# Order of a round on TensorE: values of two rounds back ahead of scores

## The reference, cut to what matters

```python
q, k, v = (split_heads(x @ W.T) for W in (Wq, Wk, Wv))      # [128, 16, 128, 32]
a = einsum('bhnd,bhmd->bhnm', q, k) * 512 ** -0.5 + 2 * adj[:, None]
a = where(any(a != 0, axis=-1, keepdims=True), a, -inf)
p = softmax(a, axis=-1)                                      # nan becomes 0
o = einsum('bhnm,bhmd->bhnd', p, v)
out = layernorm(x + merge_heads(o) @ Wo.T, eps=1e-5)
```

## Time and profile before

| | |
|---|---|
| median of three runs | 1736.4 us (1736.4 to 1737.27) |
| the profiled execution, its own time | 1735.29 us |
| its span in the profile | 1733.5 us |
| TensorE's granted clock, mean | 0.998 of full |
| busy: PE, VectorE, ScalarE, GpSimd | 99%, 92%, 79%, 55% |

### The profile page before, as it was taken

One profiled execution on the slowest core, in us unless ns is written; L12 is line 12 of the kernel. 1 busy time (PEld: TensorE's weight loads), 2 busy tenths in 40 slices (PEclk: granted clock), 3 DMA queues, 4 the chain that ended last, 5 costly groups with the idle time before them and its releaser, 6 DMA issues. The chain is left out here.

```text
span 1733.5 us, 45700 instructions
## 1 busy us (share of the span) xinstructions
PE 1708.4 (99%) x14370; PEld 1379.8 (80%) x14370; DVE 1589.5 (92%) x5815; ACT 1368.2 (79%) x5134; POOL 962.1 (55%) x1516
## 2 busy tenths in 40 slices
PE   9899999999999999999999999999999999999996
PEld 7788888888888888888888888788888888888884
DVE  7999999999999999999999999999999999999996
ACT  7787788788778877887788788778877887888775
POOL 2255556555555555565555555555655556556543
PEclk9999999999999999999999999999999999999999
DMA  6677777777777777777777777777777777777764
GB/s 213 199 225 216 226 225 227 223 216 230 226 220 225 232 218 226 214 233 224 215 231 228 223 229 215 223 225 224 234 220 216 225 225 227 226 211 234 211 200 168
DMA packets 275378, 382.59 MB, mean 221 GB/s; under 512 B 25152, under 2 KB 155200, under 8 KB 275008
## 3 DMA queue, kind: packets, MB, share of 16 engines
q1 hardware_dynamic: 274560, 378.64, 74.1%
q10 hardware_dynamic: 576, 1.05, 0.2%
HBM read 212.86 MB, written 166.72 MB: 219 GB/s over the span
## 5 line engine op out<-in xcount | busy, mean ns | idle before, releaser
L699 ACT ACTIVATE e_sb<-neg_a,neg_max 128x128 f32<-128x128 f32 x2048 | 793.2, 391 | 164.2 <-DVE neg_max L851 164.2
L851 DVE CUSTOM_DVE_ANT_0 neg_a<-ps_s,adj_sb 128x128 f32<-128x128 f32 x2048 | 442.4, 286 | 67.3 <-PE ps_s L536 67.1
L469 PE MATMUL ps_w<-xt_hi,w_lo 128*128 128x512 f32 x1020 | 414.4, 406 | 0.0
L470 PE MATMUL ps_w<-xt_lo,w_hi 128*128 128x512 f32 x1020 | 400.4, 393 | 0.0
L699 ACT ACTIVATION_READ_ACCUMULATOR e_sb<-neg_a,neg_max 128x1 f32 x2048 | 387.9, 189 | 0.0
L907 DVE STREAM_TRANSPOSE e_b<-e_sb 128x1024 f32<-128x1024 f32 x254 | 316.3, 1245 | 27.2 <-DVE e_sb L897 0.9
L349 POOL TENSOR_TENSOR o_lo<-o_sb,o_hi 128x512 fp32r<-128x512 f32 x126 | 163.8, 1300 | 289.7 <-ACT o_sb L636 289.7
L897 DVE SCALAR_TENSOR_TENSOR e_sb<-e_sb,r_inv 128x1024 f32<-128x1024 f32 x256 | 316.4, 1236 | 8.1 <-DVE r_inv L891 0.5
L859 DVE TENSOR_REDUCE neg_min<-neg_a 128x16 f32<-128x2048 f32 x128 | 292.6, 2286 | 4.4
L472 PE MATMUL ps_w<-xt_hi,w_hi 128*128 128x512 f32 x1020 | 274.0, 391 | 0.0
L469 PEld LDWEIGHTS ps_w<-xt_hi,w_lo 128*128 128x128 f32 x1020 | 191.3, 188 | 64.5 <-issue 25.3
(11 more groups left out here) (104 smaller groups left out, 2622.4 us busy)
## 6 DMA issues: line engine op xcount, KB each, us to landing
blocks<-e_b SPq DMA_DIRECT2D x1016, 128.0 KB, 2.2
e_t<-blocks SPq DMA_DIRECT2D x127, 1024.0 KB, 7.2
x_sb<-x SPq DMA_DIRECT2D x124, 256.0 KB, 4.8
out<-x_sb SPq DMA_DIRECT2D x124, 256.0 KB, 3.6
xt_raw<-xt SPq DMA_DIRECT2D x120, 256.0 KB, 4.8
adj_sb<-adj SPq DMA_DIRECT2D x32, 256.0 KB, 5.1
v_sb<-wk ACTq DMA_DIRECT2D x4, 256.0 KB, 6.4
neg_a<-xt SPq DMA_DIRECT2D x4, 256.0 KB, 5.9
```

What stands on the lines that cost most here:

```text
L469: pe.matmul(out, lhs_lo(c), rhs_hi(c), start=(c == 0), stop=False)
L470: pe.matmul(out, lhs_hi(c), rhs_lo(c), start=False, stop=False)
L699: last = act.activation(e_sb[:, i, h, :], neg_a[:, i, h, :], ACT.Exp, scale=-1.0, bias=neg_max[:, i, h:h + 1], accum_out=sums[:, i, h:h + 1])
L851: last = dve.tensor_tensor_reduce(out=neg_a[:, i, h, :], in0=ps_s[h][:, i * NODES:(i + 1) * NODES], in1=adj_sb[:, g % PAIR, i, :], scale=- ...
```

## The change

In each round of the loop, the values of two phases back are issued ahead of the scores of this phase, and the projections after both. The order in the last round, after the loop, is as it was. No instruction, wait, buffer or transfer is added or taken away.

```diff
@@ -582,9 +582,9 @@
             for kind, _, index in slots(-1):
                 first_product(kind, index)
             for f in range(LAST):
-                scores(f)
                 if f > 1:
                     values(f - 2, range(GG), ps_o)
+                scores(f)
                 for kind, g, index in slots(f):
                     if g == 0 and kind == "v":
                         first_product(kind, index)
```

## The result

The changed kernel takes 1788.6 us (median of 6 runs, 1785.3 to 1795.8) against 1736.4: 1.0302 of before, interval 1.0287 to 1.0317. It is slower by 52 us, the way and about the size that was forecast (1782, range 1756 to 1803). The profiled execution has a span of 1785.1.

The account below looks back on a forecast made before the run. TensorE, busy for 1708.4 of 1733.5 us, was taken as the bound at 13.26 us a round. 121 rounds losing 0.38 us add 46 to 1735.3, giving 1781.3, and 1.1 for the median makes 1782 (range 1756 to 1803).

Parts of the forecast that it names:

- What bounds the kernel: TensorE's work sets the round at 13.26 us; VectorE is close behind at 12.86, the move has 0.46 at the round's start.
- (a): TensorE's switches between kinds of matmul: values to scores taken as 1.01 us, all three 2.65 a round, as before.
- The dearer and the cheaper switch: Rivals on values to scores: 1.36 us gives 1811, chance 0.08; 0.81 us gives 1711, chance 0.035.
- (b): Scores end 1.01 us later in the round; VectorE's chain, the saves and the move into e_t shift with them.
- (c): Values are wanted 1.10 us earlier, at the round's start; the move's margin goes from 0.69 to -0.45 us.
- (d): A late move into e_t delays the round two later; 0.22 us a round without scatter, 0.38 taken.
- The rule carried through the old margins: Wait s(f) = max(0, u(f) - s(f-1)), u the lateness without waits, over the trace's 118 margins: 0.40 us a round.
- shorter landings in longer rounds: Fewer bytes per us go over the DMA queues in longer rounds, so 0.38 us a round was taken against 0.40.
- The sum: Rounds 6 to 126: 121 x 0.38 = 46 us on 1735.3 gives 1781.3, with the median 1782.
- Earlier rounds have fewer transfers in the queue: Reason for counting the loss only over rounds 6 to 126, with no loss added for the rounds before.
- (e): ScalarE's copies come 1.01 us later and values free e_t earlier, all at no cost.
- What was named as a sign: TensorE waits for e_t 45 to 80 us, in over half the rounds; round 13.6; busy 390 of 400; VectorE's wait 0.9.

Follow-up runs that it names:

- the early move: Against the changed kernel, SP issues the move into e_t directly behind the saves, ahead of the round's store and loads: 1741.1 us, 1.0024 of before.
- f % 4 = 0: Against the changed kernel, values ahead of scores only in the 31 rounds with f divisible by 4, the old order elsewhere: 1743.9 us, 1.0035 of before.
- even f: Against the changed kernel, values ahead of scores only in the 63 even-numbered rounds, the old order elsewhere: 1.0204 of before, +35 us.

## Why the prediction was right

*What bounds the kernel.* Right: where the move was made to land in time, or wasn't waited for, TensorE is busy for 399.7 to 400.00 of 400 us and the time is back at 1735 to 1737 us; 1741 with the early move in every round, for the reasons above. One reading is put the wrong way round there, without changing a sum: VectorE is not "slower than TensorE by almost nothing" but faster, by 0.4 us in the round shown (12.86 against 13.26).

*(a) TensorE's own work.* Right: values to scores, which no row of before showed, is 1.01 us, the value taken, and the sum is 2.65. The dearer and the cheaper switch fall.

*(b), (c) Both shifts.* Right. Either alone costs little: VectorE's late start +9 us, and values first without a late transpose two rounds before 6 us in 31 rounds. Together they use up the 0.69 us of margin. The way from the transpose to the landing is 11.87 us on average, against 11.84; so the landing did not get quicker.

*(d) The price.* That lateness comes back two rounds later is shown by the kernels with f % 4 = 0 and with even f. Its size: from the first bias of round 6 to that of round 127 it is 1603.35 us before and 1650.41 after, 47.1 us over 121 rounds, 0.389 each. The rule carried through the old margins had given 0.40; I had taken 0.38 for shorter landings in longer rounds, and that allowance was not borne out. All 47.1 us are lost by round 121. Rounds 122 to 127 lose nothing, though values wait 2.7 us in the last two of them.

*The sum* was 6.6 us short. The term that failed is "Earlier rounds have fewer transfers in the queue", by which rounds 2 to 5 were put at nothing. Their moves are indeed quicker (9.1 to 10.7 us from the transpose). But these rounds have fewer products, and VectorE's chain of 12.1 to 12.3 us sets their length, so there is less time to hide the move in: before, it landed only 0.3 and 0.1 us ahead of the scores of rounds 3 and 4, and 0.7 behind those of round 5, where the mean of the later rounds is 0.69 ahead. TensorE's timeline after:

```profile
55.70 1.08 PE L556 MATMUL ps_o<-e_t,v_sb 128*32 128x128 f32 x32 [2.37 <-DMA e_t<-blocks]
...
67.38 1.08 PE L556 MATMUL ps_o<-e_t,v_sb 128*32 128x128 f32 x32 [1.10 <-DMA e_t<-blocks]
...
81.20 1.08 PE L556 MATMUL ps_o<-e_t,v_sb 128*32 128x128 f32 x32 [3.23 <-DMA e_t<-blocks]
82.21 2.09 PE L536 MATMUL ps_s<-k_sb,q_sb 32*128 32x128 f32 x32
```

And before, where TensorE had idle time ahead of the same rounds:

```profile
54.82 1.17 PE L536 MATMUL ps_s<-k_sb,q_sb 32*128 32x128 f32 x32 [1.56 <-issue]
...
66.97 1.17 PE L536 MATMUL ps_s<-k_sb,q_sb 32*128 32x128 f32 x32 [1.58 <-issue]
```

Ahead of round 5 it was 1.75. So the three waits, 6.7 us, take the place of 4.9 us that TensorE stood anyway, and cost 1.8. Another 1.5 us are not a wait at all. The scores behind the wait of 3.23 us took 2.09 us in place of 1.17, because the granted clock had fallen to its lower level of 1.2 GHz. By windows, round 5 before, the same round after, and its part at the lower clock:

```profile
79.28:92.50 13.22, 13.22 (x112) 10.73 (x112) 12.35 (x45) 9.70 (x39) 2.80 (x2) 1.00 0.71 206
```

```profile
81.20:95.92 14.72, 14.72 (x112) 12.03 (x112) 11.96 (x44) 8.80 (x37) 2.37 (x2) 0.88 0.65 187
82.20:85.50 3.30, 3.30 (x39) 2.88 (x36) 1.41 (x12) 0.11 (x1) 0.07 (x1) 0.50 0.70 188
```

TensorE is busy throughout in both and has the same 112 matmul records. The prediction had no term for the clock. That this wait is what brought it down is not shown by a run of its own; before, the clock was 1.00 there.

With both, TensorE's round 6 starts 3.4 us later (95.92 where it was 92.50). Its bias starts at 98.18 where it started at 94.17, 4.0 us later, since in the new order it stands 0.6 further behind the start of this round. Rounds 6 to 127 are 1.1 over the predicted 46, and behind the bias of round 127 the span is 0.5 longer. Together 5.6 of the 6.6 us are in the profiled execution (4.0 + 47.1 + 0.5 is the span's 51.6); the rest lies between it and the median, 1.7 us apart where 1.1 was allowed, and in rounding.

*(e)* Right as far as the traces show: in the steady rounds of the run with the early move nothing but TensorE's own work is left, so none of the copies that now come later is missed.

*What was named as a sign.* Waits of 45 to 80 us: 52.7. A round of 13.6: 13.64. Busy 390 of 400: 390.3. VectorE's wait 0.9: 0.96. A wait in more than half of the rounds: 58 of 125, just under it.

## What to carry to other kernels

An engine that is 100% busy can still lose time from an order that adds no work: before a waiting step is moved ahead, take the margin of what it waits for at the new place, less the delay that the move gives to whatever sets that transfer off. Where the step then holds up the head of the same chain, the lateness comes back each time around, and about half of the mean lateness, with the scatter on top, is lost in every round, by the rule of (d) and as measured here. A margin is a distribution: 0.45 us of mean lateness, with 0.8 of scatter, cost 0.39 a round and not 0.22.

## What was not expected of the hardware

The time to landing of the 1 MB move is set as much by what is queued ahead of it as by its bytes. Behind a store and two or three loads of 256 KB it takes 7.3 us (median, 5.3 to 9.6); issued ahead of them 5.7; and at half the bytes, behind them, 5.6. Its scatter went as well: the standard deviation of the time to landing over rounds 6 to 123 is 0.71 us in the changed kernel and 0.21 with the move first. (From the transpose on it falls less, from 0.71 to 0.53.) A transfer on the critical loop belongs at the head of its queue where what then stands behind it can wait; in the tail of this kernel it could not.

A long wait can cost something behind it as well. In the profiled execution of the changed kernel some 3.4 us at 1.2 GHz followed the wait of 3.23 us in round 5 and cost 1.5 us; with the early move the clock was at that level from 55.9 to 59.3 us, behind a wait of 2.21 us that ended at 55.56. In rounds 6 to 125 of the changed kernel waits of up to 1.9 us are followed by no fall of the clock.
